# A transformer block pair on one core: part of the layer norm's iteration and the context's normalising product move from VectorE to GpSimd, and the plan is laid out anew

## What is computed

```python
h = layernorm(x) * (1 + ca) + sa                 # c-dependent scales, shifts and gates
x = x + ga * attention(h)                        # L0: alibi bias; L1: rotary embedding
h = layernorm(x) * (1 + cb) + sb
x = x + gb * ffn(h)                              # L0: gated mix of neighbours; L1: linear + low rank
# attention: scores = q k^T / 4, causal softmax w, ctx = w v, out = ctx @ W_proj + b
# layernorm: (x - mean) / sqrt(var + 1e-5)
```

## Time and profile before

| | |
|---|---|
| median of 3 runs | 2815.2 us (2811.31 to 2816.49) |
| the profiled execution | 2814.14 us, its span 2812.1 us |
| busy: TensorE / VectorE / ScalarE / GpSimd | 2448.3 / 2278.1 / 1711.8 / 850.1 us |
| mean granted clock of TensorE | 0.951 of full speed |

### The profile page before, as it was taken

How to read it: one execution, slowest core, us unless ns; L and a number is a source line. 1 busy time by engine, 2 the same in 40 slices (tenths; PEclk the granted TensorE clock), 3 DMA queues, 4 the chain that set the end, 5 groups by cost and what they waited for, 6 DMA issues and landing times.

```text
span 2812.1 us, 54982 instructions
## 1 busy us (share of the span) xinstructions
PE 2448.3 (87%) x18968; PEld 1041.3 (37%) x18968; DVE 2278.1 (81%) x7158; ACT 1711.8 (61%) x3458; POOL 850.1 (30%) x954
## 2 busy tenths in 40 slices
PE   6798877988989898988989989998989889887586
PEld 4223434323334333343434333443333434333223
DVE  4899747899987998978988898878989788962872
ACT  3286563676765576665766656755766657665164
POOL 3211351234222432225232342224322252225121
PEclk8799988999999999999999999999999999998789
DMA  7511125113312222322322123222232223001200
GB/s 232 149 47 31 37 72 146 53 35 98 118 49 83 78 79 91 90 69 76 106 68 80 57 90 100 77 77 73 76 93 89 69 80 104 22 30 61 86 19 16
DMA packets 142393, 218.28 MB, mean 78 GB/s; under 512 B 21190, under 2 KB 62556, under 8 KB 142052
## 3 DMA queue, kind: packets, MB, share of 16 engines
q1 hardware_dynamic: 142120, 214.77, 24.7%
HBM read 137.87 MB, written 77.89 MB: 77 GB/s over the span
## 4 chain that ended last, share of the span: by engine, by line
PE 55%; DVE 31%; ACT 7%; issue 4%; POOL 2%; DMA 1%; SPq 0%; DVEq 0%; ACTq 0%; POOLq 0%
PE ctx_ps L1627 12%; PE big L1608 11%; PE big L1545 11%; DVE small L1371 10%; PE small L1586 8%; PE big L1534 8%; DVE mx L1369 6%; PE big L1659 4%; ACT probs L1146 4%; ACT xn L1195 2%; DVE region L1439 2%; DVE stats L1314 2%; PE big L1642 2%; DVE mx L1371 2%; DVE region L1477 1%
## 5 line engine op out<-in xcount | busy, mean ns | idle before, releaser
L1146 ACT ACTIVATE probs<-big 128x512 f32<-128x512 f32 (+2 forms) x2560 | 1221.2, 563 | 509.2 <-PE big L1608 500.2
L1371 DVE CUSTOM_DVE_ANT_0 small<-small,mask 128x128 f32<-128x128 f32 (+3 forms) x2048 | 941.3, 518 | 158.2 <-PE small L1586 151.8
L1608 PE MATMUL big<-stack_q,stack_k 64*128 64x512 f16 (+3 forms) x6144 | 709.2, 331 | 65.5 <-ACT probs L1146 40.5
L1056 POOL TENSOR_SCALAR_AFFINE_SELECT probs<-probs 128x512 f32<-128x512 f32 x512 | 329.5, 653 | 1347.3 <-ACT probs L1146 1347.0
L1369 DVE TENSOR_REDUCE mx<-small 128x1 f32<-128x512 f32 x1024 | 652.3, 681 | 53.3 <-PE small L1586 45.9
L1627 PE MATMUL ctx_ps<-probs,v_ones 128*17 128x512 f32 (+3 forms) x6144 | 634.8, 501 | 8.5 <-POOL probs L1056 7.6
L1586 PE MATMUL small<-stack_k,stack_q 64*128 64x512 f16 (+3 forms) x3072 | 466.2, 341 | 195.0 <-DVE mx L1371 110.6
L1608 PEld LDWEIGHTS big<-stack_q,stack_k 64*128 64x128 f16 x6144 | 250.4, 95 | 491.9 <-issue 297.7
L1586 PEld LDWEIGHTS small<-stack_k,stack_q 64*128 64x128 f16 x3072 | 122.1, 94 | 693.2 <-DVE mx L1371 347.1
L1371 DVE DVE_READ_ACCUMULATOR2_ANT mx<- 128x1 f32 x2048 | 283.8, 139 | 0.0
L1534 PE MATMUL big<-hT,w_qkv 128*128 128x512 f32 x512 | 259.6, 623 | 0.3 <-issue 0.2
(11 more groups left out here) (93 smaller groups left out, 1913.3 us busy)
## 6 DMA issues: line engine op xcount, KB each, us to landing
image<-region SPq DMA_DIRECT2D x192, 256.0 KB
stack_q<-image SPq DMA_DIRECT2D x64, 512.0 KB, 3.7
stack_k<-image SPq DMA_DIRECT2D x64, 512.0 KB, 4.6
lo_dram<-region SPq DMA_DIRECT2D x64, 256.0 KB
w_qkv<-wqkv SPq DMA_DIRECT2D x16, 768.0 KB, 5.1
x_res<-x SPq DMA_DIRECT2D x32, 256.0 KB, 3.2
stack_q<-lo_dram SPq DMA_DIRECT2D x128, 64.0 KB, 3.9
stack_k<-lo_dram SPq DMA_DIRECT2D x128, 64.0 KB, 4.6
```

The source lines that it names most:

```text
L1056: g.affine_select(out=diag, in_=diag, compare_op=ALU.is_ge, fill=0.0, base=0, pattern=[[0, GH], [1, P]], channel_multiplier=-1).then_inc(m ...
L1146: s.activation(probs[:, n % HELD, heads, q0:], big[:, at.slot(turn), 0:len(pairs) * width] .rearrange("p (h q) -> p h q", h=len(pairs)), A ...
L1371: last = v.tensor_tensor_reduce(out=held, in0=held, in1=mask[:, BANK - width:], scale=1.0, scalar=3.0 * NEG, op0=ALU.add, op1=ALU.max, acc ...
L1608: last = te.matmul(big[:, at.slot(at.turn() + parity), j * width:(j + 1) * width], stack_k[rows, c, g * PAIR_N + pair, kt * P:(kt + 1) * P ...
```

## The change

The 12 Newton instructions of each chain and the last product go to GpSimd. The chain has 18 steps now, since GpSimd takes minus the mean and its product with 1/sqrt as two instructions (n = 16 and 17); n = 0 to 3 stay on VectorE. Part 2 of `norm` goes to GpSimd too. The semaphore `guessed` hands the guess over, `inverse_ready` the reciprocals, and `ctx_scaled` the product back to VectorE, which waits on it ahead of part 3 and ahead of the next part 0 (which overwrites `ctx_b`). The plan's model knows the new engines, and its numbers are others, so the order of nearly everything changes.

```diff
-LN_CHAIN = 17
+LN_CHAIN, LN_GUESS = 18, 4
-QK_LAGS = (0.0, 0.7758, 1.7394, 3.0788, 5.9576)
+QK_LAGS = (0.0, 0.7758, 0.9862, 2.7516, 5.9576)
-EASE, TURN_COST = 500.5758, 138.3034
+EASE, TURN_COST = 501.9056, 100.2546
-CHAIN_EASE, IDLE = 0.0000, 0.0465
+CHAIN_EASE, IDLE = 139.7521, 0.0198
+NORM_ON = ("DVE", "DVE", "POOL", "DVE")
...
-                return self.at("ln"), "DVE"
+                return self.at("ln"), "DVE" if item[4] < LN_GUESS else "POOL"
...
-            model.ready["norm"] = model.run("DVE", ready, (640, 200, 330, 640)[item[4]], 110)
+            model.ready["norm"] = model.run(NORM_ON[item[4]], ready, (640, 200, 650, 640)[item[4]], 110)
...
+                elif kind == "ln" and item[3] == "chain" and item[4] >= LN_GUESS:
+                    n, a, b = item[4:7]
+                    mean, ve_, rstd_, tmp_ = mv[:, a:b, 0], ve[:, a:b], rstd[:, a:b], tmp[:, a:b]
+                    if n == LN_GUESS:
+                        pool.wait_ge(guessed, at.now("normed", 1))
+                    else:
+                        pool.wait_ge(g_chain, links[0])
+                    if n == LN_CHAIN - 1:
+                        g.tensor_tensor(nmr[:, a:b], tmp_, rstd_, ALU.mult).then_inc(factors_ready, 1)
+                        return
+                    if n == LN_CHAIN - 2:
+                        last = g.tensor_scalar(tmp_, mean, -1.0, None, ALU.mult)
+                    elif n % 4 == 0:
+                        last = g.tensor_tensor(tmp_, rstd_, rstd_, ALU.mult)
...
+                elif kind == "norm" and item[4] == 2:
...
+                    pool.wait_ge(inverse_ready, at.now("inverse"))
+                    if at.own("ctx_ready"):
+                        pool.wait_ge(ctx_ready, at.now("ctx_ready"))
+                    g.tensor_tensor(pair[:, :, DH * (g_ % 2):DH * (g_ % 2 + 1)], own[:, :, 0:DH],
+                                    own[:, :, DH:DH + 1].broadcast_to([P, BANK // 32, DH]), ALU.mult).then_inc(ctx_scaled, 1)
...
                     if part == 0:
                         dve.wait_ge(ctx_saved, n)
-                        dve.wait_ge(v_chain, scaled_at[0])
+                        if at.own("ctx_scaled"):
+                            dve.wait_ge(ctx_scaled, at.now("ctx_scaled"))
...
-                    else:
-                        linked(at)
+                    elif part == 3:
+                        dve.wait_ge(ctx_scaled, at.now("ctx_scaled"))
```

More of the change, by code:

```diff
@@ L301, in other @@
             else:
-                self.ready["ln"] = self.ready["factors"] = self.run("DVE", begin, 75 * (item[6] - item[5]) if n == 0 else 77, 110)
+                self.ready["ln"] = self.ready["factors"] = self.run(engine, begin, 75 * (item[6] - item[5]) if n == 0 else 77, 110)
         elif kind == "mix":
@@ L592, in plan @@
                     later.append((lambda u=u, g=g, blk=blk, part=part: model.ready.get(("copied", u, g, blk), 1e18) if part == 0
[L593 removed]
+                                  else model.at("norm"), NORM_ON[part], ("norm", u, g, blk, part)))
     return out
@@ L638, in events @@
         e["modulated"] = 1
-    if kind == "norm" and item[4] == 3:
-        e["ctx_ready"] = 1
+    if kind == "norm":
+        e[("turned_ctx", "inverse", "ctx_scaled", "ctx_ready")[item[4]]] = 1
     if kind == "mix" and item[4] != 1:
@@ L1057, in step @@
                                     pattern=[[0, GH], [1, P]], channel_multiplier=-1).then_inc(masked, 1)
+                elif kind == "ln" and item[3] == "chain" and item[4] >= LN_GUESS:
[12 more added lines that the diff above has]
+                        last = g.tensor_tensor(tmp_, rstd_, rstd_, ALU.mult)
+                    elif n % 4 == 1:
+                        last = g.tensor_tensor(tmp_, tmp_, ve_, ALU.mult)
+                    elif n % 4 == 2:
+                        last = g.tensor_scalar(tmp_, tmp_, -0.5, 1.5, ALU.mult, ALU.add)
+                    else:
+                        last = g.tensor_tensor(rstd_, rstd_, tmp_, ALU.mult)
+                    links[0] += 1
+                    last.then_inc(g_chain, 1)
+                elif kind == "norm" and item[4] == 2:
+                    _, _, g_, blk, _ = item
+                    own = ctx_b[:].rearrange("p (c r) -> p c r", r=32)
+                    pair = ctx_n[:, blk].rearrange("p (c r) -> p c r", r=32)
+                    pool.wait_ge(inverse_ready, at.now("inverse"))
[3 more added lines that the diff above has]
+                                    own[:, :, DH:DH + 1].broadcast_to([P, BANK // 32, DH]), ALU.mult).then_inc(ctx_scaled, 1)
                 elif kind == "scale" and item[2] == 0:
@@ L1277, in _ @@
             CHAIN0 = 2
-            chain, scaled_at = [0], [CHAIN0]
+            chain = [0]
             def link(at, ins):
@@ L1296, in layernorm @@
                 own = x_res[:, batch % STREAMS]
-                if phase == "xn":
+                if phase == "xn" or phase == "chain" and n >= LN_GUESS:
                     return
@@ L1402, in step @@
                         dve.wait_ge(u_read, n)
[L1403 to L1410 removed]
+                        v.reciprocal(own[:, :, DH:DH + 1], own[:, :, DH:DH + 1]).then_inc(inverse_ready, 1)
+                    elif part == 3:
+                        dve.wait_ge(ctx_scaled, at.now("ctx_scaled"))
                         v.transpose(ctxT[:, g // 2, blk * BANK:(blk + 1) * BANK], ctx_n[:, blk]).then_inc(ctx_ready, 1)
```

36 lines of the change are left out of this document (11 added, 25 removed).

## The result

The changed kernel takes 2792.8 us at the median of 4 runs (2790.14 to 2793.79), the kernel before 2813.8 us (2811.31 to 2816.49): a ratio of 0.9924, 95% interval [0.9911, 0.9936]. It is faster by 0.8%, 21 us, where 47 were forecast.

A forecast was written before the change was run, and what follows sets the result against it. TensorE and VectorE were taken to hand the end to each other. Terms of -7.5 - 2.5 + 2.8 + 1.0 = -6.2 us a period, over eight periods, and +3 at the ends gave 2767 us, range 2718 to 2830.

The forecast's parts named there:

- term A: Two stretches where TensorE idles behind VectorE's held-up small instructions: -7.5 us a period, bounds 0 and -12.4.
- two stretches: Two 16.4 us slices of a period with 11.55 and 10.91 us of TensorE work, VectorE busy 15.0 and 15.9.
- no slice under 13 us: Sign of term A: no slice of a period has less than 13 us of TensorE work.
- third rival: The two stretches vanish whole, term A -12.4 and Term B -5: 2708 us; chance 0.17 for less than 2735.
- Term B: Rest of VectorE's relief, outside the two stretches: -2.5 us a period, bounds 0 and -5.
- Term D: GpSimd's longer chain makes masks late for TensorE: +1.0 us a period, bounds 0 and +3.6; +3 us once at the ends.
- Term C: Changes of shape on TensorE, 46 more a period at some 0.09 us: +2.8 us a period, bounds 0 and +4.1.
- first rival: VectorE's and GpSimd's queues tie each other up at product, masks and transpositions: slower, typically 2835 us; chance 0.15.
- second rival: Gain eaten: TensorE binds outside the two stretches, all shape changes count, hold-ups hit remaining VectorE work: 2790 to 2822 us; chance 0.15.

The follow-up runs named there:

- experiment without reads: The kernel before with each two-input product, sum or difference on GpSimd replaced by two constant writes: 2701.6 us, 0.9631.
- the pair of matmul experiments: Old order, only the chain moved, plus 196 extra 8-column matmuls: on 64 rows 2731.8 us; on the whole array, 392 more changes of shape, 2743.5 us.
- another order, at 1.0442: The changed kernel's plan numbers with a model that believes in VectorE, chain and product on GpSimd, against the kernel before: 2930.7 us, 1.0442.

## Why the prediction was right and wrong

**Where the end lies, and term A: right in its cause.** The two stretches of the earlier trace rows were hold-ups, and they left as forecast: no slice under 13 us, waits for maxima of 8.0 us a period (under 12). The experiment without reads shows the cause: the same instructions in 107 us less, and no such slices. But the sign of no slice under 13 us came with the new layout's help. In the old order with the new engines one slice of the second stretch still has 3.8 us of idle time, and the granted clock is 0.89 in it; it had 5.5.

One reading behind term A was wrong. The two slices are not those with the most GpSimd work; the period's last one has more than either, and an ordinary amount of TensorE's:

```profile
1617.60:1634.00 16.40, 14.40 (x110) 5.55 (x111) 16.20 (x47) 6.31 (x14) 14.26 (x15) 1.00 0.38 119
```

So the amount of GpSimd's work alone doesn't make a bad slice; that it is a matter of which VectorE instructions meet it fits the rows, but no run sets it apart. The third rival (all of it goes) was not so far off for the move alone: with the chain moved and the old order the time is 2731 and 2737 us, against its 2708.

**The size of A, B and D together: right in sum, by two errors.** By its steps the prediction had -7.5 - 2.5 + 1.0 = -9.0 us a period, eight periods and +3, that is -69 us, and the old order with the new engines gives -66. But a period fell more and the ends hardly at all. The gates' product of `w_ffn` is issued 16 times; between its fourth and fourteenth start lie ten units, five periods. That stretch shrank by 61.9 us, 12.4 a period; what lies before and after it changed by -7.6 and +2.5 us. Counting eight periods for five was wrong, and A and B were too small by as much. That the sum fits within 3 us is luck.

**Term C is the step that failed: "+2.8 a period" for the new layout.** It priced the layout as changes of shape alone, 314 x 0.09 us (its two rows differ by 0.08), of which it took two thirds, 2.8 us in each of eight periods or 22 us in all. On top of the move the layout cost 45 us. In the five periods it is (1596.7 - 1554.6) / 5 = 8.4 us each, three times the term. Of the 43 us between the two spans TensorE's busy time makes 31 (2464.7 - 2433.4) and its idle time 12. The changes of shape themselves are some 10 us at the price that the pair of matmul experiments gives. The rest lies in how the work is ordered: waits for exponentials go from 52.1 to 66.7 us, for masks from 9.5 to 19.3, for `ctx_u` from 0.8 to 8.1, and the projections and transposes take 17.6 us longer, the projections beginning behind another shape 181 times instead of 134. The prediction named the new layout's order only by what could be counted in it, and gave it no price for being another order. With 45 in place of 22 us it would have said 2790.

That an order drawn anew has a price of its own is shown: with both parts on GpSimd, the old order, the changed kernel's, the one with the true chain time, and those of the other plans lie between 2747 and 2931 us. Which single decisions of the changed kernel's order lose the 35 us that this price doesn't explain stays open. That the order meets more of the hold-ups is excluded, and putting the product back doesn't recover them.

**Term B and VectorE's busy time.** 190 us of groups leave, but the busy time fell by 122, not to 2090 or 2110 us. With the old order it fell by 150: instructions overlap at their ends, so the sum of a group counts some time twice. In the new layout it fell by 28 less, though the groups' sum is only 6 us above that of the old order (2494.6 and 2488.2): the instructions stand further apart and overlap less. The prediction took the sum of groups for a share of the union.

**Term D: about right in its sizes.** A link of 0.28 us against 0.25, a chain of 3.9 us against 3.5, a product of 0.645 us against 0.73; GpSimd's busy time rose by 176 us, not 220. Matmuls' waits for masks of 3.1 us a period are under the 6 named. The 2.6 us that the prediction started from are idle time of weight loads; matmuls had no such wait in the period, so the 3.1 are all new, three times the 1.0 us of the term. Most of it comes with the layout: in the whole kernel these waits rise from 7.6 to 9.5 us with the move in the old order, and to 19.3 in the changed kernel. The plan's model had a chain of 2.6 us, and this was named as a shortfall of 0.9 us; it is 1.3, and correcting it moved the time by 0.45%.

**The first rival** didn't come in this kernel: the transposition waited for the product 19.5 us in all, about 2 us a period against the 10 named. One half of it, the masks, came in another order, at 1.0442. **The second rival** is what happened in its range of times, and not by its sign: it wanted TensorE above 305 us a period, which has 299. Its reading that the gain is eaten on TensorE's side is borne out by 31 of the 43 us of the layout; the other 12 are idle time, above all waits for ScalarE and for masks.

The Trainium skill (GPSIMD Engine Reference, Engine selection) would keep two-input elementwise work on VectorE. The chain's links are indeed slower on GpSimd, 0.20 against 0.161 us at the median, and the product 0.645 against 0.424; yet the time fell by 2.6% with the chain moved. By the rule of the Trainium skill (SBUF — State Buffer, Who interferes with whom) a VectorE instruction with two SBUF inputs contends with a GpSimd instruction that reads SBUF and not with one that only writes it. The experiment without reads agrees: none of 58 such instructions was held up by a constant write, and VectorE's busy time fell by 107 us.

## What to carry to other kernels

Small dependent instructions can be moved from a queue where an engine waits behind them to one that is slower but free, and here the gain was the hold-ups they no longer meet (some 70% of it) more than their own time. It depends on the order: in one plan the same move made the kernel slower. When a change also lays out the schedule anew, measure the move in the old order first: here it gave 66 us, and the new order took 45 back. Price a new order by what the same work costs in several orders (here 0.9764 to 1.0442 of the time before), not by the one feature that can be counted in it.

## What was unexpected in the hardware

With GpSimd's two-input instructions replaced by shorter constant writes, VectorE's busy time fell by 107 us (2278.1 to 2171.6) and the kernel's time by 3.7%. A constant write held up none of 58 small two-input instructions of VectorE and 31 of 42 one-input ones. A tiny 128x8 operation costs 0.20 us on GpSimd, a quarter more than VectorE's median of 0.161. A change of shape on TensorE between 64 rows and the whole array is 0.055 us of its busy time and 0.033 us of the kernel's, though the first projection matmul behind one is shown 0.105 us longer than the next.
